# Graph network layers on one core: where VectorE adds the bias of the second product at a change of block

## The reference

```python
for l in range(L):                       # L = 5
    h_in = h + vn[batch]
    emsg = relu(h_in[src] + edge_attr @ We[l] + be[l])
    agg = segment_sum(emsg, dst, num_segments=N)
    t = h_in + agg
    t = relu(t @ W1[l] + b1[l]) @ W2[l] + b2[l]
    t = (t - bn_m[l]) * (bn_g[l] * rsqrt(bn_v[l] + EPS)) + bn_b[l]
    if l < L - 1:
        t = relu(t)
    h = t + h_in
```

## Time and profile before

| what | us |
|---|---|
| median of three runs | 9367.71 (9363.5 to 9368.68) |
| profiled execution, its own time | 9374.53 |
| its span, first to last instruction | 9372.7 |
| PE busy / POOL busy / DVE busy / ACT busy | 6152.2 / 5231.5 / 3611.3 / 1609.9 |
| mean granted clock of PE | 0.786 of full speed |

### The profile page before, as it was taken

The page is one execution under the profiler, slowest core; times in us unless marked ns, Lnnn a source line. Parts: engine busy times, 40 slices in busy tenths (PEclk is TensorE's granted clock), DMA queues, the critical chain, the costliest instruction groups (busy, mean ns, idle before and its releaser), DMA issues. The chain is left out here.

```text
span 9372.7 us, 114718 instructions
## 1 busy us (share of the span) xinstructions
PE 6152.2 (66%) x28483; PEld 4699.3 (50%) x28484; DVE 3611.3 (39%) x5667; ACT 1609.9 (17%) x3223; POOL 5231.5 (56%) x5128
## 2 busy tenths in 40 slices
PE   3667667765776667556856783656666666666666
PEld 2556545654565456445644562444453453454345
DVE  4445434443443334334543453545561121122123
ACT  1222212221222112212200013332330000000000
POOL 3555465546554655555557744543316676766666
PEclk8889878887888788778877886777786776777677
DMA  4333333333333333333333315554423332332333
GB/s 121 105 100 99 99 106 97 96 96 104 102 93 97 105 101 96 98 105 100 105 92 87 89 58 190 197 177 158 144 86 92 95 93 87 93 94 83 90 95 89
DMA packets 434518, 987.02 MB, mean 105 GB/s; under 512 B 124176, under 2 KB 210832, under 8 KB 417936
## 3 DMA queue, kind: packets, MB, share of 16 engines
q0 software_dynamic: 245760, 673.51, 25.1%
q1 hardware_dynamic: 128816, 194.88, 6.3%
q10 hardware_dynamic: 59744, 116.68, 3.8%
HBM read 845.23 MB, written 139.46 MB: 105 GB/s over the span
## 5 line engine op out<-in xcount | busy, mean ns | idle before, releaser
L371 POOL DMA_INDIRECT ring<-node_table,idx x4608 | 4711.4, 1022 | 3306.6 <-issue 2091.2
L382 PE MATMUL psE<-ring,shared 128*128 128x256 f32 x3072 | 1027.7, 471 | 449.0 <-issue 338.3
L987 DVE TENSOR_TENSOR ring<-ring,psE 128x1024 f32<-128x1024 f32 x640 | 762.5, 1218 | 1048.8 <-issue 436.1
L382 PEld LDWEIGHTS psE<-ring,shared 128*128 128x128 f32 x3072 | 660.7, 229 | 791.6 <-issue 502.0
L263 DVE SCALAR_TENSOR_TENSOR shared<-iota,block_start,dst_f 128x1024 f32<-128x1024 f32 x352 | 450.8, 1286 | 1395.0 <-remote 817.4
L1364 POOL DMA_INDIRECT ring<-att_table,idx x512 | 519.2, 1014 | 764.8 <-ACT idx L1568 496.1
L851 ACT ACTIVATE ring<-ring 128x1024 f32<-128x1024 f32 x640 | 661.9, 1060 | 937.2 <-DVE ring L987 673.8
L397 PE MATMUL psE<-ring,stk 128*128 128x256 f32 x1984 | 545.5, 429 | 248.8 <-DVE stk L263 133.6
L691 PE MATMUL psE<-we_stk,stk 128*128 128x256 bf16 x2560 | 394.5, 296 | 451.1 <-issue 161.8
L382 PE MATMUL psAT<-ring,shared 128*128 128x256 f32 x2560 | 653.1, 410 | 47.9 <-issue 47.9
L382 PE MATMUL psAT<-ring,S 128*128 128x256 f32 x2560 | 649.6, 409 | 30.1 <-issue 30.0
(11 more groups left out here) (356 smaller groups left out, 7018.0 us busy)
## 6 DMA issues: line engine op xcount, KB each, us to landing
ring<-node_table,idx POOLq DMA_INDIRECT x4608
rows_table<-ring SPq DMA_DIRECT2D x64, 1072.0 KB
ring<-rows_table ACTq DMA_DIRECT2D x64, 1072.0 KB
stk<-stack_table SPq DMA_DIRECT2D x128, 512.0 KB
node_table<-tab ACTq DMA_DIRECT2D x251, 128.0 KB
stack_table<-stk SPq DMA_DIRECT2D x64, 256.0 KB
ring<-att_table,idx POOLq DMA_INDIRECT x512
tab<-in_x ACTq DMA_DIRECT2D x35, 128.0 KB
```

Of the source, the lines that this page charges most:

```text
L371: nc.gpsimd.indirect_dma_start(ring[:, q, 0:gw], None, table, bass.IndirectOffsetOnAxis(ap=idx[:, RING * half + q:RING * half + q + 1], ax ...
L382: ins = nc.tensor.matmul(bank, hots[:, u, :], ring[:, U * ob + u, 0:D], start=False, stop=True, skip_group_check=True)
L987: nc.vector.tensor_tensor(ring[:, q:q + 4, 0:D], ring[:, q:q + 4, 0:D], psE[:, 4 * D * g:4 * D * g + 4 * D].rearrange("p (u f) -> p u f", ...
```

## The change

One call moves within DVE's turn, from behind the one-hots to the head:

```diff
                                     bank = sums_in(psAT, dve, bank_dve)
 
+                                    scaled(n)
                                     dve.wait_ge(further_done, nd)
                                     take_sums(n, b, bank).then_inc(sums_read, 1)
                                     further_hots(h, c)
-                                    scaled(n)
                                     dve.drain()
                                     finish(n, block_back(dve, last_blk, 4), block_back(dve, last_blk, 5))
```

## The result

The changed kernel takes **9319.47 us** (median of 5 runs, 9288.49 to 9335.62), beside 9367.71 us for the kernel before (median of 5 runs, 9347.88 to 9379.42). The sign was right, the size was not, and the traces show that most of the gain came by another way than the one that was costed.

The account below looks back on a forecast made before the run. No engine's busy time was taken as the bound, but a chain handing over from engine to engine; 14 us (long waits) + 6 (short waits) = 20 off 9374.5, and the runs' median 6.8 below the profiled one, gave 9348 us, range 9322 to 9371.

Parts of the forecast that it names:

- The sign: Whole kernel: predicted faster, 20 us off the profiled execution.
- PE finds its operand ready: Second product (L721), first kind of turn: DVE's addition ends at 1767.47, PE starts at 1768.91 without a wait.
- the turns without a wait: 93 of 155 turns and all of layer 0: addition moves into DVE's wait for the transposes; costed at nothing.
- the short waits: 46 turns where PE reaches L721 as the addition is just ending: 11.4 us in all, half taken, 6 us.
- Nobody waits for that: Turns without a wait: DVE is through with `finish` 0.42 us sooner, but the next link is ACT's relu; no gain.
- the long waits: 16 turns in layers 1 to 4, PE waiting 2.1 to 12.5 us at L721: main term, 14 us, bounds 0 to 15.7.
- What moves: DVE's turn: one 0.41 us instruction with its wait and signal; at the head it holds DVE no longer; no cost.
- The third rival: PE's further products: later further one-hots become what PE waits for, 26 us slower in 62 turns, 9394 us; chance 0.08.
- the smaller of 2.0 and the time from relu's end to the transposes: Rule for gain per long-wait turn: six turns give 2.0 us each, ten give 0.02 to 1.3.
- The first rival: L721 behind long waits: PE starts warm, clock and issue recover, at most 29 us on top, 9319 us; chance 0.13.
- The second: PE's unfinished work lies behind its records, so starting L721 earlier gains nothing: 9368 us, give or take 3; chance 0.17.
- The closing test: PE's waits at the second product: prediction wrong in kind if another number of turns than 62 has PE waiting.

Follow-up runs that it names:

- e13: The kernel before itself, unchanged, run again for a trace on the occasion that also ran the change: 9297.74 us, ratio 0.9995 to the kernel before.
- e14: The change itself, unaltered, run for a trace on the same occasion as the repeated kernel before: 9181.01 us, ratio 0.9859 to the kernel before.
- e3: Kernel before with one tiny write (one element per partition) added at the head of DVE's turn: 9354.87 us, ratio 0.9989.
- e9: Kernel before with two branches on the octet group in layers 1 to 4, both guarding the bias addition at its old place: 9263.35 us, ratio 0.9975.
- e17: Kernel before with one more addition of 0.42 us and a drain just ahead of the bias addition at its old place: 9358.06 us, ratio 0.9991.
- e4: The change itself, unaltered, measured once more against the kernel before: 9310.65 us, ratio 0.9945.
- e10: The change plus two branches on the octet group in layers 1 to 4, both at the head, against the kernel before: 9131.33 us, ratio 0.9845.
- e11: The change itself, unaltered, measured against the kernel before on another occasion: 9143.79 us, ratio 0.9853.
- e18: Against the kernel before, bias addition between the two halves of the further one-hots, still behind the sums; a repeat run: 9312.83 us, ratio 0.9935.
- e7: Against the kernel before, addition ahead of L263 where a change of block follows, at a turn's end where another turn does: 9191.85 us, ratio 0.9889.
- e15: Kernel before with gathers in layers 1 to 4 fetching 64 of 256 columns: 9299.28 us, ratio 1.0004.

## Why the prediction was wrong

**The step that failed** is the reading of the earlier trace rows: "PE finds its operand ready", and, built on it, "Nobody waits for that" and "I cost it at nothing". It took a product of PE that starts without idle time for one whose operand was ready. In the first trace of before the addition's signal released PE's queue in all 61 such turns (80 us of waiting in all; none of 61 after), and in 30 of the 43 turns with a short wait (100 us, where PE's rows show 12; 46 us after). So the sum had the turns without a wait at 0 and the short waits at 6 by what the array's rows show alone. From e13 to e14 these two kinds gave 13 and 86 of the 128 us of layers 1 to 4, and the main term, the long waits, 23, which can't be told from the spread of the traces.

**What moves: right.** Nothing was added to the path, and the addition stands where it was said. The wait for `f_result` did hold DVE at the head, in 16 of the 155 turns of the loop in the profiled execution of after, up to 6.7 us. But `f_turned` came at least 1.8 us later each time, so it held DVE no longer than the wait behind it, as the text says. The third rival (slower by the further one-hots) did not show: L397 doesn't wait for DVE in the turns looked at. One count is wrong, at no cost to the sum: of the 93 turns without a wait 31 are layer 0's, so layers 1 to 4 have 62 of 124.

**Long waits, 14 us: not found.** The rule was "the smaller of 2.0 and the time from relu's end to the transposes". It took the 4.2 us of rows 6 as work that starts earlier if L721 does; in the long-wait turn shown above L721 did start sooner behind L263, and L712 took longer. The 16 turns took 647 us before and 654 after, 684 in e13 and 660 in e14. Five traces with the old order (before, e3, e9, e13, e17) have 647 to 692, five of the change (after, e4, e10, e11, e14) 638 to 670, so a gain of 14 us can be neither seen nor ruled out there. e18 has the gain without shorter waits, e7 no more gain without long ones.

**Short waits, 6 us: these turns gave the most, for another reason.** The 46 small gaps did go, all of them (12 us of waits became none). The 43 of these turns that lie between two others shortened by 38 us in the first pair of traces (1300.7 to 1262.7 us), and by 86 us from e13 to e14. The 38 alone prove little, as the five traces with the old order have 1240 to 1301; the 1161 to 1176 of e10, e11 and e14 lie clear of them. It isn't the gaps in PE's rows that were paid back, since e17 makes them more than twice as large at no cost. Most of these turns span two octets, and both octets can take either rhythm: in e13 four of the 43 take less than 26 us, in e14 21. A turn can fall into slow records, as in this piece of the kernel before (PE and POOL, behind a gap at L721 of less than 0.1 us):

```profile
1495.91 1.97 PE L721 MATMUL psV<-w_odd,hT 128*128 128x256 f32 x8
...
1497.72 1.28 PE L712 MATMUL psO<-tT,w_sb 128*128 128x128 f32 x10
...
1499.64 0.95 POOL L371 DMA_INDIRECT ring<-node_table,idx  x1 [0.30 <-issue]
1500.32 0.27 PE L712 MATMUL psO<-tT,w_sb 128*128 128x128 f32 x1 [1.33 <-issue]
...
1501.75 0.27 PE L712 MATMUL psO<-tT,w_sb 128*128 128x128 f32 x1 [1.16 <-issue]
...
1503.19 0.27 PE L712 MATMUL psO<-tT,w_sb 128*128 128x128 f32 x1 [1.17 <-issue]
```

Ten products take 1.28 us, and each of the next 1.43. On average over the 43 turns L712 took 7.4 us before and 4.9 after, L397 8.6 and 9.7. But L712 took 3.6 and 3.0 in e13 and e14, where the gain was larger.

**Turns without a wait, 0 us: the failed step.** Of the 61 between two others one holds several octets (55 to 74 us, at random); the other 60 took 845.8 us before and 837.3 after, 839.5 in e13, 826.7 in e14 and 806.5 in e18. Between 11.3 and 12.8 us lie none of them before and in e13, 8 after, 20 in e14, 18 in e18. In e14 a part of that is lost again: four other turns grew past 17 us. The cover that the text gave, ACT's relu nine microseconds later, is off the path of PE's queue. PE seemed to have 1.44 us to spare between the end of the addition (1767.47) and L721 (1768.91), but its queue was at the wait 0.8 us before that end.

The same holds in the short rhythm. In the turn of e14 the one-hots end at 3604.50 + 0.75 = 3605.25, and the old order would have ended the addition at about 3605.6; PE's array started L721 at 3604.24, and its queue had passed the wait for `f_used` at 3602.04. In all 20 short turns of e14, and in all 14 of e11 and 8 of after, the queue passes that wait before the old order would have ended the addition, by 0.8 us or more (median 1.8 to 2.2). The old place would hold it each time. Had one looked at the array's rows alone, only 9 of e14's would show a conflict.

**The first rival** (clock and issue recover) is nearest in time, 9319 to 9333 us, by luck, and wrong in kind: the granted clock over the span is 0.785 after and 0.786 before, and behind the long wait shown L721 still takes 3.75 us. **The second** (PE's work behind its records) named the right gap, relu 4.6 us behind L712, but drew the wrong end from it. The gap is the late signal `f_hid`, not PE's products: `further_done`, sixteen products on, comes with it. Over the 50 turns of 13.8 to 15.4 us in the first trace of before, relu starts 1.65 us (median) after the record of the octet's last gather ends, and 1.46 in e13. In e14's 19 turns of 11.3 to 12.7 us it starts 2.1 us ahead of it.

**The closing test** of the prediction, "wrong in kind if another number of turns than 62 has PE waiting", came true: 46 short waits became none, and the long ones (over 1 us) went from 16 to 18. The latter number is one of the run: it is 14 in e4, the same kernel.

**What stays open.** How a queue that gets `f_used` earlier leads to a signal `f_hid` that gets out early: the experiments show that the place of the addition decides whether the short rhythm occurs, and the trace shows the hold at the old place, but no run shows the link between the two, nor what holds the signals back. And what sets the two levels of time of one kernel, 9364 and 9300 us on the same chip, with which the gain goes: 50 us at the one, 120 to 145 at the other. The prediction had no way to see the second from one trace, and no term for it.

## What to carry to other kernels

An engine whose rows show no idle time may still wait: before costing a moved step at nothing, look when the engine's queue passes the wait for it (here line 719), and not only when the product behind starts. Where turns take one of two lengths (here 14.3 and 12.4 us), count how many take each; a sum of waits saved doesn't forecast a count. When an engine starts late for no reason that the timeline names, compare the time of the signal with that of its neighbours. And repeat both kernels on a second occasion before believing the size of a gain of half a per cent.

## What the runs showed of the hardware

- PE's signals can come long after the records of the products that set them. `f_hid` came between 0.3 and 12.8 us after the start of the last record of L712 (median 4.2, 120 turns of before), and in 40 of 50 like turns it came within 0.2 us of a signal whose products lie 3.35 us behind. `f_result` came 13.8 us after the last record of L721 in one turn of after (1589.98 to 1603.80).
- PE's queue passes a wait well before the array starts the product behind it: 1.6 us (median) in those 50 turns, 3.1 us in the 45 of after.
- The pace of PE's records changes by a factor of ten within a line with nothing to wait for: 0.12 us each, then 1.43 (L712 above). Steps of over 0.6 us between products of L382, L397, L712 and L721 hardly occur in the first 10 us of an unbroken run of gathers (share 0.00 in e13) and make up 0.3 to 0.4 of those from 15 to 20 us (before, after, e13 to e18 alike). DVE's register and semaphore instructions slow down in the same stretches, to about 0.70 us each: 424 of them last 0.6 to 0.8 us in layers 1 to 4 before, 277 after, 425 and 264 in e13 and e14. Moving 30% fewer bytes in all gathers together (e15) left the time as it was.
- One kernel on one chip took 9300 us (9262 to 9326) on one occasion and 9364 (9339 to 9394) on the next, while executions of one occasion stay together; a change of order gave 0.55% at the one level and 1.4 to 1.5% at the other.
